# Attention in a four-layer kernel: the bonus turned from a contiguous tile, two value quarters and one copy moved in the order of the engines

## The chip, the cores and the metric

The kernel runs on one core of a Trainium2 chip (trn2). The metric is the device time of one execution in microseconds, the median of several runs. A profiled execution has a time of its own and a span (first to last instruction) inside it.

## The reference

Four layers, each with a layer norm ahead, a layer norm behind and a residual. Only the first one is touched by the change. It is an attention over B=32 sequences of T=256 positions, D=128, 16 heads with 4 numbers per key and 64 per value:

```
Q = normalize(x @ W_q.T); K = normalize(x @ W_k.T); V = x @ W_v.T      # per head
Qn = normalize(Q @ W_nudge); scores = Qn @ K.T * 0.5
s = sigmoid(3 * K @ simple_roots.T)                                   # 4 numbers a head and key
cw = products of s or 1-s for the 16 corners; k_bonus = cw . chamber_bonus[head]
scores += k_bonus[key]; causal mask; attn = softmax(scores); out = (attn @ V) @ W_out.T
x = x + layernorm(out)
```

The other layers are a gated feed-forward, a tanh recurrence and a mixture of 32 experts; they run after the attention in the same program and are the same in both kernels.

## The kernel before, in words

The attention works on one sequence (a block) at a time, and every engine runs the same software pipeline over blocks: step(b, f, n, m, z, y, par) does scores and weighted values for block b, the preparation of keys, queries and values for f = b+1, norm and the q/k projection for n = b+2, input statistics for m = b+3, the output projection for z = b-1 and the closing norm for y = b-2. The order on each engine is written out by hand, and the engines wait for each other by semaphores. The loop (Fori) holds two blocks in its body; six blocks at the start and five at the end are written out.

- TensorE (L568 to L645, in rounds' step): scores(b, p) for the head pairs p = 0 to 7 (L478), weighted(b, g) for the groups g = 0 to 3 (L500, with row sums L508), weighted(z, 3) between scores(b, 0) and scores(b, 1). Between them: the transposes of xn (L574), the q/k projection L586 from xnT, four quarters of the values, values(f, 0..3) (L551, three matmuls each, into the bank back), spread_out (L522), the turn of the bonus (L600, the matmul of k5_wide's fifth column with the identity), the turn of qkn (L613), the turn of the running maximum cmax (L620), the rotation L627, the turns of k_aug and q_aug (L560) and the output projection (L536).
- GpSimd: copy of the keys into k5 (L412), bonus() as a tree of eight, four, two and one products (L367 to L379), the last of which writes column 4 of k5_wide (a tile of 144 rows of 5 floats); the masks 0 to 7 (L323, an affine select over two heads pairs of probabilities), three of them between the steps of bonus(); split() of k5 and q5 into three bf16 parts (L332, L336), the rows of k_aug and q_aug (L423 to L451), and 1/sqrt of the variances (L350, L352).
- ScalarE: the exponentials, weights(b, h, h+1) (L655), copies of PSUM banks: copy_out (L665), copy_values (L673), xnT (L684), squares (L689), q_augT (L722), y_sb (L727).
- VectorE: reciprocal of the row sums of z and its bf16 parts (L788 to L797), sum of squares and three Newton steps (L828 to L760), normalise (L806), qkn (L840), bonT (L846: the turned bonus out of PSUM), the running maximum cmax over keys by a scan (L849), q5 (L855, L864) and the rest of the norms.

A score's key bonus and the query's running maximum are extra columns of k5 and q5. mask p waits for the exponentials of its two heads, weighted(b, g) waits for mask 2g+1, scores(b, p) waits for the exponentials of pair p-1, and reciprocal(z) waits for the sums of weighted(z, 3).

Of the kernel before, what the change touches and what calls it, by code (L numbers as in the profile page):

```python
# [14 lines left out]
P = 128  # L15
# [77 lines left out]
def attention_layer(nc, x, w_qk, w_v, w_rot, w_out, bonus0, bonus_step, x1_d, mix, mix_d, room, row_buf, sorted_d):  # L93

    with ExitStack() as ctx:
# [6 lines left out]
        def sem(name):  # L102
# [53 lines left out]
        q_augT = [sb(f"q_augT{i}", [P, GROUPS, T], BF16) for i in range(2)]  # L156
        k_augT = [sb(f"k_augT{i}", [P, GROUPS, T], BF16) for i in range(2)]
        bonT = sb("bonT", [HEADS, T])
        cmax = sb("cmax", [P, T])
        views = 10 * HID  # L160
        val = [room[:, views + i * SPAN:views + (i + 1) * SPAN].rearrange("p (i h v) -> p i h v", i=TT, h=HEADS)
               for i in range(2)]
# [31 lines left out]

        names = ("w", "const", "xa", "stat_a", "mv_a", "ve", "rstd", "xn", "p_xnT", "xnT", "p_qk", "sq1", "ss1",
                 "ssg1", "roots", "qkn", "p_qkT", "qkT", "p_rot", "sq2", "ek", "qraw", "ss2", "ssg2", "ek1",
                 "sg", "q4", "kcopy", "bon", "p_bonT", "bonT", "cmax", "p_cmax", "q5", "ksplit", "qsplit", "kaug",
                 "qaug", "p_kaT", "p_qaT", "kaT", "qaT", "p_v", "val", "p_score", "prob", "masked", "p_out", "raw",
                 "p_sum", "rec", "rec_high", "rec_rest", "rec_mid", "rec_parts", "rest_row", "wv_split", "low_sel", "back_row", "back_r", "xnT_high", "xnT_low", "p_bc", "onT", "p_y",
                 "y", "stat_y", "mv_y", "yn", "xr", "x1", "x1_out", "mix_w", "mix_split_v", "mix_split_g", "mix_const", "blank", "fill")  # L200
# [3 lines left out]
        BON = 11  # L204
        RSQ = 10
        N_IDENT = 4
        N_CONST = 22

        ctx.callback(clear, nc, list(s.values()))
        block = ctx.enter_context(nc.Block(no_gpsimd_drain=True))  # L210
# [68 lines left out]
        def _(pool):  # L279
# [11 lines left out]
            def late_constants():  # L291
                const(pool.memset(q_aug[:], 0.0))
                const(pool.memset(k5_wide[:], 0.0))
                const(pool.memset(cmax[:], 0.0))
                const(pool.memset(k_aug[:], 0.0))
                const(pool.memset(q_aug[:, :, 27:30], 1.0))
                const(pool.memset(k_aug[:, :, 24:27], 1.0))
                for row, fill, base in ((high_row, 1.0, 0), (mid_row, -1.0, -GROUPS), (low_row, -1.0, -2 * GROUPS)):

                    const(pool.memset(row[:], 0.0))  # L300
                    const(pool.affine_select(out=row[:].rearrange("p (g j) -> p g j", j=GH),
                                             in_=row[:].rearrange("p (g j) -> p g j", j=GH),
                                             compare_op=ALU.not_equal, fill=fill, base=base,
                                             pattern=[[-1, GROUPS], [-AUG, GH]], channel_multiplier=1))
                const(pool.memset(pick[:], 0.0))
                flat = pick[:].rearrange("p g c -> p (g c)")
                const(pool.memset(flat[:, 0:GROUPS * (AUG + 1) - AUG:AUG + 1], 1.0))
                for row in (GROUPS, 2 * GROUPS):
                    const(pool.memset(flat[:, row:row + GROUPS * (AUG + 1) - AUG:AUG + 1], 1.0))
                const(pool.memset(pick[:, :, 3 * GROUPS:], 1.0))  # L310
                pool.memset(row_buf[:], 0.0).then_inc(s["blank"], 1)
                pool.wait_ge(s["blank"], 1)
                pool.memset(row_buf[:, :, ROW_ID:ROW_ID + 1], 1.0).then_inc(s["blank"], 1)
                pool.wait_ge(s["w"], 96)
                const(pool.tensor_tensor(bond[:], bond[:], bon0[:], ALU.subtract))
# [38 lines left out]
            def bonus(n, between):  # L354

                wait_apart(pool, s["sg"], n + 1, s["const"])
                wait_apart(pool, s["p_bonT"], n, s["const"])
                def did(ins):
                    did.c += 1
                    ins.then_inc(s["bon"], 1)  # L360
                    wait_apart(pool, s["bon"], BON * n + did.c, s["const"])
                did.c = 0
                def sig(r, w):
                    return sg[:, :, :, r:r + 1].to_broadcast([P, TT, HEADS, w])
                step_b = bond[:].rearrange("p (o h) c -> p o h c", o=1).to_broadcast([P, TT, HEADS, 8])
                base_b = bon0[:].rearrange("p (o h) c -> p o h c", o=1).to_broadcast([P, TT, HEADS, 8])
                did(pool.tensor_tensor(bt[0][:], sig(0, 8), step_b, ALU.mult))  # L367
                did(pool.tensor_tensor(bv[0][:], bt[0][:], base_b, ALU.add))
                between(0)
                for r in range(1, 4):  # L370
                    pair = bv[r - 1][:].rearrange("p i h (c two) -> p (i h) c two", two=2)
                    w = 8 >> r
                    t = bt[r][:].rearrange("p i h c -> p (i h) c")
                    sr = sg[:].rearrange("p i h r -> p (i h) r")[:, :, r:r + 1].to_broadcast([P, TT * HEADS, w])
                    did(pool.tensor_tensor(t, pair[:, :, :, 1], pair[:, :, :, 0], ALU.subtract))
                    did(pool.tensor_tensor(t, t, sr, ALU.mult))
                    out = bv[r][:].rearrange("p i h c -> p (i h) c") if r < 3 \
                        else k5_wide[:, 0:TT * HEADS, DH:DH + 1]
                    did(pool.tensor_tensor(out, t, pair[:, :, :, 0], ALU.add))  # L379
                    if r != 2:  # L380
                        between(1 if r == 1 else 2)

# [24 lines left out]
            def step(b, f, n, m, z, y, par):  # L407
                if isinstance(m, int) and m == 1:
                    late_constants()
                if f is not None:  # L410
                    wait_apart(pool, s["qkn"], f + 1, s["const"])
                    pool.tensor_scalar(k5[:, :, :, 0:DH], qkn[:, :, HEADS:, :], 1.0, 0.0,  # L412
                                       ALU.mult, ALU.add).then_inc(s["kcopy"], 1)
                    bonus(f, lambda p: mask(b, p))
                    mask(b, 3)
                    wait_apart(pool, s["kcopy"], f + 1, s["const"])
                    wait_apart(pool, s["p_kaT"], f, s["const"])
                    split(k5, k_part, "ksplit", f)
                    wait_apart(pool, s["ksplit"], STEPS_K * (f + 1), s["const"])

                    kp = k_part[:].rearrange("p k r c -> p r k c")
                    rows = k_aug[:].rearrange("p r (m c) -> p r m c", c=DH)
                    pool.tensor_scalar(rows[:, :, 0:3, :], kp[:, :, :, 0:DH], 1.0, 0.0, ALU.mult, ALU.add)  # L423
                    pool.tensor_scalar(rows[:, :, 3:5, :], kp[:, :, 0:2, 0:DH], 1.0, 0.0, ALU.mult, ALU.add)
                    pool.tensor_scalar(rows[:, :, 5, :], kp[:, :, 0, 0:DH], 1.0, 0.0, ALU.mult, ALU.add)
                    pool.tensor_scalar(k_aug[:, :, 27:30], kp[:, :, :, DH], 1.0, 0.0,
                                       ALU.mult, ALU.add).then_inc(s["kaug"], 1)
                else:
                    for p in range(4):
                        mask(b, p)  # L430
                        if isinstance(b, int) and b == B - 1:
                            split_weight("h2", p)
# [27 lines left out]
        def _(pe):  # L460
# [104 lines left out]
            def step(b, f, n, m, z, y, par):  # L565
# [30 lines left out]
                if f is not None:  # L596
                    wait(pe, s["bon"], BON * (f + 1))
                    wait(pe, s["qaT"], f)
                    for i in range(TT):
                        mm = pe.matmul(turned[:, i * P:(i + 1) * P], k5_wide[:, i * HEADS:i * HEADS + P, DH], ident[:],  # L600
                                       start=True, stop=True)
                    mm.then_inc(s["p_bonT"], 1)
                values(f, par, 2)

                scores(b, par, 4)
                weighted(b, par, 1)
                scores(b, par, 5)

                spread_out(z, 1)
                if n is not None:  # L610
                    wait(pe, s["qkn"], n + 1)
# [1 line left out]
                        mm = pe.transpose(front[:, i * P:(i + 1) * P], qkn[:, i].rearrange("p h c -> p (h c)"),  # L613
                                          ident[:])
                    mm.then_inc(s["p_qkT"], 1)
                values(f, par, 3)
                if f is not None:
                    wait(pe, s["cmax"], f + 1)
                    for i in range(TT):
                        mm = pe.matmul(turned[:, T + i * HEADS:T + (i + 1) * HEADS], cmax[:, i * P:(i + 1) * P],  # L620
                                       ident[:, 0:HEADS], start=True, stop=True)
                    mm.then_inc(s["p_cmax"], 1)
                spread_out(z, 2)
                if n is not None:
                    wait(pe, s["qkT"], n + 1)
# [22 lines left out]
        def _(act):  # L648
# [27 lines left out]
            def step(b, f, n, m, z, y, par):  # L676
                weights(b, 0, 1)
                copy_out(z, 1 - par, 3)
                weights(b, 2, 3)

                if n is not None:
                    wait(act, s["p_xnT"], n + 1)
                    wait(act, s["p_v"], 4 * (n - 1))
                    act.activation(xnT[par][:], front[:, 0:T], ACT.Copy).then_inc(s["xnT"], 1)  # L684
                copy_values(f, par, 0)
                if n is not None:
                    wait(act, s["p_qk"], n + 1)
# [8 lines left out]
                copy_out(b, par, 0)  # L696
                weights(b, 6, 7)
                copy_values(f, par, 1)
                copy_values(f, par, 2)

                weights(b, 8, 9)
                copy_out(b, par, 1)
                weights(b, 10, 11)
                if n is not None:
                    wait(act, s["p_qkT"], n + 1)
                    act.activation(qkT[:], front[:, 0:T], ACT.Copy).then_inc(s["qkT"], 1)
# [1348 lines left out]
```

## Time and profile before

| | |
|---|---|
| median of 3 runs | 1771.08 us (1771.04 to 1773.08) |
| profiled execution | 1771.21 us |
| its span | 1769.4 us |
| busy share of the span: TensorE, its weight loads, VectorE, ScalarE, GpSimd | 93%, 70%, 75%, 50%, 57% |
| attention half | about the first 780 us |
| granted TensorE clock, mean | 0.973 |

How to read it: the share of an engine is an average over all layers. In a time line of one engine, each row is one instruction or a run of equal ones with its start and length; a note in brackets is the idle time ahead of it and what ended that. Starts of neighbouring matmuls overlap, so the time that a group holds TensorE is the distance from its start to the next group's start. Gaps below 0.15 us have no note.

### The profile page before, as it was taken

The page shows a single profiled execution, that of the slowest core. Times are in us where ns is not written, and L with a number is a line of the kernel's source. Part 1 is how long each engine was busy: PE and PEld are TensorE (multiplying, and loading weights), DVE is VectorE, ACT ScalarE, POOL GpSimd, SP SyncE. Part 2 cuts the span into 40 slices and gives each one's busy share as a digit, 9 for nine tenths or more (in the row PEclk, how much of TensorE's full clock was granted, in tenths as well). Part 3 has the DMA queues.
Part 4 walks back from the last instruction along what each step waited for, and adds up shares of the span by engine and source line. Part 5 has one row for each costly group of instructions (what it writes and reads, how often), then busy time and mean ns, then how long its engine had stood idle before and what let it go on. Part 6 is the DMA issues. An engine that isn't in the chain of part 4 may idle for free.

```text
span 1769.4 us, 47120 instructions
## 1 busy us (share of the span) xinstructions
PE 1639.8 (93%) x14871; PEld 1231.4 (70%) x14871; DVE 1318.6 (75%) x3869; ACT 889.9 (50%) x2003; POOL 1005.7 (57%) x1782
## 2 busy tenths in 40 slices
PE   3999999999999999859999999999999999689996
PEld 2677777777777777537778888878787886555553
DVE  5688888888888888645567777777777775758886
ACT  2666666666666666514444444444444443224443
POOL 5888888888888888722233333333333333327777
PEclk8999999999999999969999999999999999699998
DMA  1001111111111113010120000000000002534441
GB/s 42 11 29 55 54 54 54 54 54 54 54 54 54 54 54 104 14 36 13 50 81 22 31 28 29 27 30 29 26 30 28 26 25 75 178 123 133 133 132 41
DMA packets 78259, 95.96 MB, mean 54 GB/s; under 512 B 7046, under 2 KB 62995, under 8 KB 78160
## 3 DMA queue, kind: packets, MB, share of 16 engines
q1 hardware_dynamic: 70992, 77.91, 13.8%
q0 software_dynamic: 7168, 16.87, 2.7%
q8 instruction: 46, 0.75, 0.2%
q14 instruction: 53, 0.43, 0.1%
HBM read 53.14 MB, written 43.69 MB: 55 GB/s over the span
## 4 chain that ended last, share of the span: by engine, by line
PE 40%; DVE 7%; issue 4%; POOL 2%; DMA 1%; ACT 1%; DVEq 0%; POOLq 0%; SPq 0%; ACTq 0%
PE main L1329 6%; PE main L1331 5%; PE main L1338 5%; PE main L1487 4%; PE yp L1409 3%; PE xi L1244 2%; PE main L1269 2%; PE main L1282 2%; PE main L1393 2%; PE main L1396 1%; PE main L1394 1%; PE route L1501 1%; PE xi L1501 1%; PE turn L1237 1%; PE yp L1509 1%
## 5 line engine op out<-in xcount | busy, mean ns | idle before, releaser
L655 ACT ACTIVATE wgu<-score 128x384 f32<-128x384 f32 x512 | 223.2, 489 | 80.1 <-PE score L478 78.6
L1329 PE MATMUL main<-hT_high,h_high 128*128 128x512 f32 x512 | 221.2, 432 | 0.9 <-ACT hT_high L1586 0.9
L1331 PE MATMUL main<-hT_high,h_low 128*128 128x512 f32 x512 | 201.3, 393 | 0.0
L500 PE MATMUL outp<-wgu 128*32 128x256 f32 (+1 forms) x4096 | 194.5, 331 | 5.4 <-POOL wgu L323 4.3
L323 POOL TENSOR_SCALAR_AFFINE_SELECT wgu<-wgu 128x512 f32<-128x512 f32 x256 | 167.1, 658 | 46.1 <-ACT wgu L655 28.2
L500 PEld LDWEIGHTS outp<-wgu 128*32 128x32 f32 x4096 | 115.9, 110 | 70.6 <-issue 22.1
L1338 PE MATMUL main<-hT_low,h_high 128*128 128x512 f32 x512 | 138.3, 391 | 0.1
L1894 DVE SCALAR_TENSOR_TENSOR th<-th,main 128x512 f32<-128x512 f32 x64 | 43.9, 686 | 114.5 <-ACT th L1613 114.5
L536 PE MATMUL back<-wout,wgu 128*128 128x128 f32 x1024 | 128.6, 280 | 0.0
L536 PEld LDWEIGHTS back<-wout,wgu 128*128 128x128 f32 x1024 | 121.9, 195 | 0.4
L1227 POOL DMA_INDIRECT out<-res,idx x96 | 96.8, 1008 | 44.1 <-issue 40.5
L1244 PEld LDWEIGHTS xi<-state,wh_sb 128*128 128x128 f32 x512 | 93.1, 195 | 39.2 <-ACT state L1536 22.9
L1536 ACT ACTIVATE state<-xi,bias 128x32 f32<-128x32 f32 x256 | 73.2, 286 | 86.7 <-PE xi L1244 85.6
L1338 PEld LDWEIGHTS main<-hT_low,h_high 128*128 128x128 f32 x512 | 96.2, 188 | 21.8 <-DVE hT_low L1848 0.8
L508 PE MATMUL total<-wgu,pick 128*32 128x256 f32 (+1 forms) x2048 | 108.2, 329 | 0.0
L1170 POOL TENSOR_SCALAR bve_f<-bmv_f 128x4 f32<-128x4 f32 x16 | 7.7, 484 | 174.7 <-DVE bmv_f L1691 174.7
L1165 POOL TENSOR_TENSOR hT_low<-wgu,hT_high 128x512 fp32r<-128x512 f32 x64 | 83.0, 1297 | 42.0 <-ACT wgu L1578 41.4
L1329 PEld LDWEIGHTS main<-hT_high,h_high 128*128 128x128 f32 x512 | 97.0, 189 | 13.6 <-ACT hT_high L1586 1.4
L1577 ACT ACTIVATE hT_high<-main,sc 128x512 fp32r<-128x512 f32 x64 | 44.0, 688 | 124.0 <-PE main L1338 124.0
L1331 PEld LDWEIGHTS main<-hT_high,h_low 128*128 128x128 f32 x512 | 97.1, 190 | 11.7 <-issue 0.2
L1487 PE MATMUL main<-wgu,xgT 128*128 x192 | 100.2, 604 | 3.3 <-DVE hid_g L1947 2.4
L665 ACT ACTIVATE wgu<-outp 128x512 f32<-128x512 f32 x128 | 76.5, 598 | 48.1 <-PE outp L500 45.7
(295 smaller groups left out, 4353.9 us busy)
## 6 DMA issues: line engine op xcount, KB each, us to landing
sorted_d<-row_buf SPq DMA_DIRECT2D x26, 772.0 KB, 3.7
xg<-sorted_d SPq DMA_DIRECT2D x48, 386.0 KB
wgu<-in_gate_up SPq DMA_DIRECT2D x4, 2048.0 KB
xa<-in_x SPq DMA_DIRECT2D x32, 128.0 KB, 3.5
xr<-in_x SPq DMA_DIRECT2D x32, 128.0 KB, 3.3
x_d<-x SPq DMA_DIRECT2D x32, 128.0 KB, 1.8
x1c<-x_d SPq DMA_DIRECT2D x16, 256.0 KB, 2.7
x1v<-x_d SPq DMA_DIRECT2D x16, 256.0 KB, 2.7
```

What stands on the lines that cost most here:

```text
L323: pool.affine_select(out=blocks, in_=blocks, compare_op=ALU.is_ge, fill=0.0, base=0, pattern=[[0, 4], [1, P]], channel_multiplier=-1).then ...
L500: m = pe.matmul(outp[AUG * j:AUG * (j + 1), p % 2, k * P:T], val[par][:, k, h, v:v + AUG], weights(h, k), start=(k == 0), stop=(k == 1), t ...
L508: m = pe.matmul(total[AUG * j:AUG * (j + 1), k * P:T], pick[:, g, :], weights(GH * g + j, k), start=(g == 0 and k == 0), stop=(g == GROUPS ...
L536: m = pe.matmul(back[:, i * P:(i + 1) * P], onT[1 - par][:, c, i * P:(i + 1) * P], wout[:, c, :], start=(c == 0 and i == 0), stop=(c == PA ...
L655: act.activation(prob[:, h // 2 % (RING // 2), :, h % 2, :], score[h % BANKS][:, 0:SC].rearrange("p (c q) -> p c q", q=P), ACT.Exp).then_i ...
L1165: pool.tensor_tensor(hT_part[1][1][:, m, :], hT[1][:, m, :], hT_part[1][0][:, m, :].bitcast(F32), ALU.subtract).then_inc(s["h2_low"], 1)
L1227: pool.indirect_dma_start(out=out_rows[:, :], out_offset=bass.IndirectOffsetOnAxis(ap=idx[k][:, n:n + 1], axis=0), in_=res[k][:, n, :], in ...
L1244: pe.matmul(xi[:, o:o + B], wh_sb[:], state[:, prev:prev + B], start=False, stop=(t == STEPS - 1), skip_group_check=True).then_inc(s["p_st ...
L1329: pe.matmul(main[m % 2][:, :], w[0][:, k, m * P:(m + 1) * P], src[0][:, k, :], start=(k == 0), stop=False)
L1331: pe.matmul(main[m % 2][:, :], w[1][:, k, m * P:(m + 1) * P], src[0][:, k, :], start=False, stop=False)
L1338: mm = pe.matmul(main[m % 2][:, :], w[0][:, k, m * P:(m + 1) * P], src[1][:, k, :], start=False, stop=(k == HC - 1))
L1487: pe.matmul(main[2 * (r % 2) + i][:, :], xgT[r % 2][:, i * P:(i + 1) * P], wgu[:, bass.ds(e, 1), :].rearrange("p o i -> p (o i)"), start=T ...
```

## The change

On GpSimd, the last product of the bonus goes to a new tile bonus_row (144 contiguous floats a partition, zeroed at the start, so that there is one constant more), and a new tensor_scalar copies its 32 columns into column 4 of k5_wide, with a semaphore bon_k of its own that the k split waits for. On TensorE the turn of the bonus (L600) takes its weights from bonus_row; values(f, par, 2) moves from ahead of scores(b, par, 4) to behind scores(b, par, 5); values(f, par, 3) moves from ahead of the turn of cmax to behind it. On ScalarE the copy of xnT moves ahead of weights(b, 2, 3), and copy_values(f, par, 2) moves behind weights(b, 10, 11).

```diff
+        bonus_row = sb("bonus_row", [P, P + HEADS])
@@
-        N_CONST = 22
+        N_CONST = 23
@@ GpSimd
+                const(pool.memset(bonus_row[:], 0.0))
@@ GpSimd, bonus()
                     out = bv[r][:].rearrange("p i h c -> p (i h) c") if r < 3 \
-                        else k5_wide[:, 0:TT * HEADS, DH:DH + 1]
+                        else bonus_row[:, 0:TT * HEADS].rearrange("p (r o) -> p r o", o=1)
                     did(pool.tensor_tensor(out, t, pair[:, :, :, 0], ALU.add))
+                    if r == 3:
+                        pool.tensor_scalar(k5_wide[:, 0:TT * HEADS, DH], bonus_row[:, 0:TT * HEADS], 1.0, 0.0,
+                                           ALU.mult, ALU.add).then_inc(s["bon_k"], 1)
@@ GpSimd, step
                     wait_apart(pool, s["kcopy"], f + 1, s["const"])
+                    wait_apart(pool, s["bon_k"], f + 1, s["const"])
                     wait_apart(pool, s["p_kaT"], f, s["const"])
                     split(k5, k_part, "ksplit", f)
@@ TensorE, step
                     for i in range(TT):
-                        mm = pe.matmul(turned[:, i * P:(i + 1) * P], k5_wide[:, i * HEADS:i * HEADS + P, DH], ident[:],
+                        mm = pe.matmul(turned[:, i * P:(i + 1) * P], bonus_row[:, i * HEADS:i * HEADS + P], ident[:],
                                        start=True, stop=True)
                     mm.then_inc(s["p_bonT"], 1)
-                values(f, par, 2)
 
                 scores(b, par, 4)
                 weighted(b, par, 1)
                 scores(b, par, 5)
 
+                values(f, par, 2)
                 spread_out(z, 1)
@@ TensorE, behind the turn of qkn
-                values(f, par, 3)
                 if f is not None:
                     wait(pe, s["cmax"], f + 1)
@@
                     mm.then_inc(s["p_cmax"], 1)
+                values(f, par, 3)
                 spread_out(z, 2)
@@ ScalarE, step
                 copy_out(z, 1 - par, 3)
-                weights(b, 2, 3)
-
                 if n is not None:
                     wait(act, s["p_xnT"], n + 1)
                     wait(act, s["p_v"], 4 * (n - 1))
                     act.activation(xnT[par][:], front[:, 0:T], ACT.Copy).then_inc(s["xnT"], 1)
+                weights(b, 2, 3)
+
                 copy_values(f, par, 0)
@@
                 copy_values(f, par, 1)
-                copy_values(f, par, 2)
 
                 weights(b, 8, 9)
                 copy_out(b, par, 1)
                 weights(b, 10, 11)
+                copy_values(f, par, 2)
```

## Rows read from the trace of the kernel before

**Rows 1.** Busy time (instructions) by engine, TensorE clock and DMA, block A's window
```profile
core 0: us, PE busy (x) PEld busy (x) DVE busy (x) ACT busy (x) POOL busy (x), PEclk, DMA share, GB/s
379.87:402.42 22.55, 22.18 (x318) 16.29 (x314) 19.01 (x45) 14.52 (x34) 18.75 (x42) 1.00 0.17 57
```
**Rows 2.** Time line of TensorE in block A: start us, length us, engine, line, operation
```profile
379.87 0.34 PE L478 MATMUL score<-q_augT,k_augT 32*128 32x256 bf16 x4
380.14 0.44 PE L574 MATMUL front<-ident,xn 128*128 128x128 f32 x2
...
381.44 0.71 PE L586 MATMUL front<-wqk,xnT 128*128 128x128 f32 x4 [0.17 <-ACT xnT L684]
...
382.62 1.51 PE L500 MATMUL outp<-wgu 128*32 128x256 f32 x32 [0.20 <-POOL wgu L323]
...
386.01 1.05 PE L600 MATMUL turned<-ident,k 128*128 128x128 f32 x4
386.82 0.48 PE L551 MATMUL back<-wv_high,xnT_high 128*128 128x512 f32 x1
...
387.96 1.51 PE L500 MATMUL outp<-wgu 128*32 128x256 f32 x32
...
390.06 0.34 PE L478 MATMUL score<-q_augT,k_augT 32*128 32x256 bf16 x4
...
390.69 0.48 PE L551 MATMUL back<-wv_high,xnT_high 128*128 128x512 f32 x1
...
391.47 0.51 PE L620 MATMUL turned<-ident,cmax 128*128 128x16 f32 x4
```
**Rows 3.** Time line of VectorE in blocks A and B
```profile
380.10 1.76 DVE L788 RECIPROCAL rec<-total 128x256 f32<-128x256 f32 x1 [0.78 <-PE total L508]
...
386.13 0.70 DVE L758 TENSOR_TENSOR root_t<-sums,root 128x96 f32<-128x96 f32 x1
...
390.12 0.95 DVE L849 TENSOR_TENSOR_SCAN cmax<-bonT 16x256 f32<-16x256 f32 x1
...
402.60 1.76 DVE L788 RECIPROCAL rec<-total 128x256 f32<-128x256 f32 x1 [1.07 <-issue]
...
408.31 0.26 DVE L758 TENSOR_TENSOR root_t<-sums,root 128x96 f32<-128x96 f32 x1
...
412.08 0.96 DVE L849 TENSOR_TENSOR_SCAN cmax<-bonT 16x256 f32<-16x256 f32 x1
```
**Rows 4.** Time line of TensorE in block B and at its end
```profile
413.75 0.51 PE L620 MATMUL turned<-ident,cmax 128*128 128x16 f32 x4
...
424.69 0.34 PE L478 MATMUL score<-q_augT,k_augT 32*128 32x256 bf16 x4
```
**Rows 5.** Time line of GpSimd in blocks A and B
```profile
381.85 0.64 POOL L323 TENSOR_SCALAR_AFFINE_SELECT wgu<-wgu 128x512 f32<-128x512 f32 x1 [0.31 <-POOL bv L379]
...
385.33 1.39 POOL L323 TENSOR_SCALAR_AFFINE_SELECT wgu<-wgu 128x512 f32<-128x512 f32 x2 [0.31 <-POOL k L379]
...
404.04 0.64 POOL L323 TENSOR_SCALAR_AFFINE_SELECT wgu<-wgu 128x512 f32<-128x512 f32 x1 [0.31 <-POOL bv L379]
...
408.36 0.70 POOL L323 TENSOR_SCALAR_AFFINE_SELECT wgu<-wgu 128x512 f32<-128x512 f32 x1 [0.20 <-ACT wgu L655]
```
**Rows 6.** All instructions of L600, L620, L788: duration ns min/median/max, first and last start
```profile
L600 PEld LDWEIGHTS turned<-ident,k x128: 295/316/321, 28.6 to 722.1; 128*128 128x128 f32 x128
L620 PEld LDWEIGHTS turned<-ident,cmax x128: 187/192/333, 34.2 to 727.0; 128*128 128x128 f32 x128
L788 DVE RECIPROCAL rec<-total x32: 1757/1758/1758, 66.7 to 760.1; 128x256 f32<-128x256 f32 x32
```
**Rows 7.** Groups of GpSimd instructions, 200 to 700 us: busy us, mean ns, idle
```profile
L412 POOL TENSOR_SCALAR k<-qkn 128x128 f32<-128x128 f32 x22 | 6.6, 301 | 0.0
```
**Rows 8.** Time line of ScalarE in block A
```profile
380.24 0.87 ACT L655 ACTIVATE wgu<-score 128x384 f32<-128x384 f32 x2 [0.29 <-PE score L478]
381.00 0.39 ACT L684 ACTIVATE xnT<-front 128x256 f32<-128x256 f32 x1
381.31 0.60 ACT L673 ACTIVATE wgu<-back 128x512 f32<-128x512 f32 x1
```

More of the change, by code:

```diff
@@ L196, in attention_layer @@
                  "ssg1", "roots", "qkn", "p_qkT", "qkT", "p_rot", "sq2", "ek", "qraw", "ss2", "ssg2", "ek1",
-                 "sg", "q4", "kcopy", "bon", "p_bonT", "bonT", "cmax", "p_cmax", "q5", "ksplit", "qsplit", "kaug",
+                 "sg", "q4", "kcopy", "bon", "bon_k", "p_bonT", "bonT", "cmax", "p_cmax", "q5", "ksplit", "qsplit", "kaug",
                  "qaug", "p_kaT", "p_qaT", "kaT", "qaT", "p_v", "val", "p_score", "prob", "masked", "p_out", "raw",
```

## Prediction

> **What bounds the kernel now.** The change touches only the attention half, the first 780 us of the profiled execution. I read first the busy time of one stretch of the attention loop, then the time lines of TensorE, VectorE, GpSimd and ScalarE in two neighbouring blocks. The loop body holds two blocks, and they differ a little: block A runs from 379.87 to 402.42 us (22.55 us), block B from 402.42 to 424.69 us (22.27 us), both counted from the matmuls of scores(b, 1), a point that I call S1. Their mean is 22.41 us; the ends of the window in [rows 1] are two neighbouring S1. TensorE is busy for 22.18 of the 22.55 us of block A. What the reader is to see in its time line [rows 2] is how small its named waits are: 0.17 us for xnT ahead of L586 and 0.20 us for mask 1 ahead of weighted(0). In a loop this tight the question is which ring of waits has the least slack. There are three.
>
> TensorE alone: 22.27 us in block B, with the xnT wait in it.
>
> VectorE and TensorE: the reciprocal L788 waits for the sums that end just ahead of S1. It starts 0.23 us behind S1 in A and 0.18 us in B, and VectorE then works almost without a gap to the end of the running maximum L849, which is at 390.12+0.95 = 391.07 us in A and 412.08+0.96 = 413.04 us in B [rows 3]. That is S1+11.20 and S1+10.62. TensorE takes that maximum at L620, at 391.47 and 413.75 us, S1+11.60 and S1+11.33 [rows 2, 4]. From there to the next S1 TensorE needs 402.42-391.47 = 10.95 us in A and 424.69-413.75 = 10.94 us in B. So this ring has a slack of a few tenths only: 0.4 us in A and 0.7 us in B, less what it takes from the maximum to the first matmul.
>
> GpSimd: in its time line nearly every gap is a wait for its own last result, as the 0.31 us ahead of mask 2 in A. The one clear wait for another engine is 0.20 us ahead of mask 3 in B [rows 5]. Two blocks take 44.82 us, so its own work fills (44.82-0.20)/2 = 22.31 us a block. GpSimd is nearly as tight as TensorE.
>
> **The turn of the bonus from a contiguous tile.** The weight loads of L600, which step over five floats, take 316 ns; those of L620, contiguous and of the same size, take 192 ns [rows 6]. L600's four instructions now hold TensorE for 386.82-386.01 = 0.81 us [rows 2]. With loads of 192 ns I scale that by 192/316 and get 0.49, a saving of 0.32 us a block; the bounds are 0 and 4*(316-192) ns = 0.50 us. On TensorE's own path that would be 32*0.32 = 10.2 us. But it lies between S1 and L620, the stretch that the VectorE chain covers, so it only makes TensorE arrive earlier at a wait.
>
> **The copy back into k5 on GpSimd.** One tensor_scalar of 128x32. L412, the same operation on 128x128, has a mean of 301 ns [rows 7]; L379 to mask 2 has a gap of 0.31 us [rows 5] that comes from two waits in a row, and the copy sits between these two. Its cost is between 0 (hidden by the second wait) and 0.30 us; I take 0.05 us, since the copy is a quarter of L412's size and the second wait is worked off while it runs. Its wait bon_k ahead of the split has behind it the k split, k_aug and with it the turn of k_aug on TensorE, but it is passed during mask 3 (about 0.65 us of work), so it costs 0. By the forecast below GpSimd gets 0.5 us of slack a block, so even 0.30 us would not reach the end. The extra memset (128x144) runs once at the start, 0 to 0.3 us; I take 0.
>
> **The turned input ahead of exponentials 2 and 3.** The exponentials now start at 380.24 us, S1+0.37 [rows 8]. The transposes of xn end at 380.14+0.44 = 380.58 us [rows 2], so xnT can start at about S1+0.78 and takes 0.31 us of ScalarE's time (from 381.00 to the next start at 381.31; its record says 0.39). The two exponentials then run from S1+1.09 to S1+1.96. Mask 1, which needs them, can start at S1+2.09 (0.13 us for the semaphore, as from the end of mask 1 at 382.49 to weighted(0) at 382.62) and ends at S1+2.73. Now it ends at S1+2.62 in A and S1+2.26 in B [rows 5]. So this move takes away the 0.17 us wait at L586 and puts weighted(0) at S1+2.86, 0.1 to 0.4 us later than now. Both lie under the VectorE chain as well.
>
> **Quarter 2 of the values one block of scores later, quarter 3 behind the maximum.** The first swaps places only: one quarter goes from ahead of weighted(1) to behind scores(5). The second, which the short name of the change doesn't mention, is the one that counts: values(f, 3) goes from ahead of L620 to behind it. A quarter takes 391.47-390.69 = 0.78 us [rows 2]. TensorE reaches L620 earlier by that, where the maximum isn't ready, and has 0.78 us more to do behind it.
>
> **The sum.** A new block is: S1 to the end of the maximum, then to the first matmul of L620, then the rest. From the end of the maximum to L620 I take 0.26 us (0.13 us for the semaphore and 0.13 us of the first weight load of 0.19 us, which nothing hides now; bounds 0.1 and 0.4 us). The rest is the present one plus 0.78 us. Block A: 11.20+0.26+10.95+0.78 = 23.19 us, 0.64 us more than now. Block B: 10.62+0.26+10.94+0.78 = 22.60 us, 0.33 us more. The mean is +0.485 us. The reciprocals are 32 [rows 6]; the last three belong to blocks in which the next-but-one input is missing and VectorE's chain is short, so 29 blocks count: 29*0.485 = +14.1 us. The profiled execution took 1771.2 us (its span 1769.4 us and 1.8 us around it), the median of the runs is 1771.1 us, so the two bases are the same within 0.1 us. 1771.2+14.1 = **1785.3 us**.
>
> **What may make the VectorE chain longer or shorter.** It is the same list of instructions in A and B and yet takes 10.97 us in one and 10.44 us in the other. The same L758 takes 0.70 us where it starts beside a GpSimd mask and 0.26 us elsewhere [rows 3]. I see about 1.3 us of such lengthening in A and 0.8 us in B, so the chain lies between 9.65 and some 11.3 us, by how it falls against GpSimd's masks and splits. The Trainium skill ("SBUF — State Buffer", SBUF: two separate sides) calls the port pair that the two engines share an exclusive lock, given to whichever instruction starts first, the other fully blocked; the trace agrees with its 0.70 against 0.26 us.
>
> **The rivals.** (1) The collisions get worse. With mask 1 from S1+2.09 on, masks 2 and 3 begin near S1+5.6 and S1+6.35, and the root steps, which run from S1+5 to S1+8, meet both masks and the first subtraction of the split. Each meeting costs 0.2 to 0.5 us, which gives every block at least A's chain: 23.0 to 23.2 us, +0.6 to +0.8 us, 1788.6 to 1794.4 us. The page's lock is the rule by which this goes, and by it both blocks would get the longer chain.
> (2) No change. If the chain loses nearly all of its collisions (9.65 us), its ring falls to 0.23+9.65+0.26+11.73 = 21.87 us and others bind. TensorE by way of exponentials 2 and 3: weighted(0) at S1+2.86; weighted(1) 4.24 us later by TensorE's work (387.96-382.62 = 5.34, less 0.78, less 0.32) and, by mask 3, 4.36 us behind the end of mask 1, so S1+7.1; scores(5) 2.10 us later and L620 another 1.41 us later [rows 2], S1+10.6; with 11.73 us that is 22.35 us. GpSimd's own 22.31+0.05 = 22.36 us agrees. So 22.35 us, -0.06*29 = -2 us, 1769.5 us.
> (3) Faster. If besides that GpSimd's lengthened steps shrink by 0.2 us and the exponentials come 0.15 us earlier than I reckon, the block is 22.2 us: -0.2*29 = -6 us, 1765 us. A full gain of TensorE's 0.32+0.17 us a block (14 us, 1757 us) would need all rings to give way. Against both stands GpSimd's work of 22.31 us.
> (4) The turn isn't faster from a contiguous tile. Then TensorE reaches L620 at S1+10.9 instead of S1+10.6, still at the maximum or 0.1 us behind it in B: 1785 to 1788 us. The 192 ns of L620's loads speak against it.
>
> **How the numbers follow.** A measurement of this kernel can tell about 0.2% (3.5 us) from no change. Forecast, 1779 to 1789 us: 0.50. Rival 1: 0.17. Rival 4: 0.05. Rival 2: 0.17. Rival 3: 0.11. The faster side is rival 3 (0.11), no change is rival 2 without a tail and the low edge of the forecast (0.15), the rest is slower (0.74). The range must reach over rival 2 and most of rival 1: 1768 to 1795 us.
>
> **What would show it.** In the trace after, TensorE should have an idle time ahead of L620 that ends with VectorE's running maximum, 0.3 to 0.8 us in every block; the distance from that matmul to the next S1 should be 11.7 us; mask 1 should wait for the exponentials; GpSimd should show waits for ScalarE ahead of mask 0; weight loads of the bonus turn should be near 192 ns. The forecast is wrong if the maximum ends before S1+10.4 us, so if the chain sheds its collisions, or if the stretch behind L620 grows by less than 0.78 us because something in it was waiting unseen.

## The result and the profile after

The changed kernel takes 1787.65 us (median of 4 runs, 1782.7 to 1789.6), the kernel before 1771.06 us beside it; the ratio is 1.0091, with a 95% interval of 1.0075 to 1.0106. It is slower, by 16.6 us. Its profiled execution took 1782.7 us with a span of 1780.6 us.

The change touches the attention half only, so the cleanest measure is the time from the first to the last y_sb copy, one per block. Its row for the kernel before and for the changed one (minimum, median and maximum length in ns, then first and last start in us):

```profile
L727 ACT ACTIVATE y_sb<-back x32: 384/384/385, 86.8 to 774.5; 128x256 f32<-128x256 f32 x32
```
```profile
L733 ACT ACTIVATE y_sb<-back x32: 384/384/386, 86.1 to 788.0; 128x256 f32<-128x256 f32 x32
```

That is 687.7 us before and 701.9 us after, +14.2 us; the forecast was +14.1 us. The other 2.4 us of the 16.6 us can't be placed: they are less than what the time outside these copies scatters by. The same changed kernel, profiled again, had 702.1 us between the copies and 1787.7 us in all, against 701.9 and 1782.7 us. The two traced runs, before and changed, differ by 1782.7-1771.2 = 11.5 us only.

In the changed kernel a block takes 22.91 to 22.96 us from one S1 (the matmuls of scores(b, 1)) to the next, 22.93 us on the mean of six, against 22.41 us. TensorE's time line after, the block that starts at 386.52 us, answers to [rows 2]:

```profile
386.52 0.34 PE L484 MATMUL score<-q_augT,k_augT 32*128 32x256 bf16 x4
...
387.78 0.71 PE L592 MATMUL front<-wqk,xnT 128*128 128x128 f32 x4
388.55 0.34 PE L484 MATMUL score<-q_augT,k_augT 32*128 32x256 bf16 x4
389.46 1.51 PE L506 MATMUL outp<-wgu 128*32 128x256 f32 x32 [0.58 <-POOL wgu L325]
...
392.86 0.61 PE L606 MATMUL turned<-ident,bonus_row 128*128 128x128 f32 x4
393.40 0.34 PE L484 MATMUL score<-q_augT,k_augT 32*128 32x256 bf16 x4
393.71 1.51 PE L506 MATMUL outp<-wgu 128*32 128x256 f32 x32
...
397.11 0.38 PE L619 MATMUL front<-ident,qkn 128*128 128x128 f32 x2
397.63 0.62 PE L625 MATMUL turned<-ident,cmax 128*128 128x16 f32 x4
398.10 0.48 PE L557 MATMUL back<-wv_high,xnT_high 128*128 128x512 f32 x1
...
409.48 0.34 PE L484 MATMUL score<-q_augT,k_augT 32*128 32x256 bf16 x4
```

The reader is to see three things. The wait for xnT ahead of the projection (now L592) is gone, and a wait of 0.58 us for mask 1 ahead of weighted(0) stands in its place. The turn of the bonus holds TensorE for 393.40-392.86 = 0.54 us instead of 0.81 us. And between the turn of qkn and the turn of the maximum there is a hole: 397.11 to 397.63 us, where the two transposes of qkn hold TensorE for 0.14 us. VectorE's time line, which answers to [rows 3], shows what ends it:

```profile
386.75 1.76 DVE L794 RECIPROCAL rec<-total 128x256 f32<-128x256 f32 x1 [1.21 <-PE total L514]
...
392.35 0.74 DVE L764 TENSOR_TENSOR root_t<-sums,root 128x96 f32<-128x96 f32 x1
393.12 0.57 DVE L765 SCALAR_TENSOR_TENSOR root_u<-root_t,root 128x96 f32<-128x96 f32 x1
...
396.69 0.88 DVE L855 TENSOR_TENSOR_SCAN cmax<-bonT 16x256 f32<-16x256 f32 x1
```

The maximum ends at 396.69+0.88 = 397.57 us, S1+11.05, and TensorE's turn of it starts 0.06 us later. From there to the next S1 are 409.48-397.63 = 11.85 us, against 10.95 us in [rows 2, 4]. The waits of the weight loads from 200 to 700 us say the same for all 22 blocks (columns: waiting line, what it waited for, us in total, times, longest):

```profile
PEld outp L506 <- POOL wgu L325: 9.8, 22, 0.7
PEld turned L625 <- DVE cmax L855: 9.1, 22, 0.5
```

GpSimd, which answers to [rows 5], now waits for the exponentials ahead of mask 1, and its new copy L383 stands ahead of masks 2 and 3:

```profile
388.63 0.71 POOL L325 TENSOR_SCALAR_AFFINE_SELECT wgu<-wgu 128x512 f32<-128x512 f32 x1 [0.64 <-ACT wgu L661]
...
391.65 0.25 POOL L381 TENSOR_TENSOR bonus_row<-bt,bv 128x32 f32<-128x32 f32 x1
392.07 0.35 POOL L383 TENSOR_SCALAR k<-bonus_row 128x32 f32<-128x32 f32 x1 [0.16 <-POOL bonus_row L381]
392.35 1.24 POOL L325 TENSOR_SCALAR_AFFINE_SELECT wgu<-wgu 128x512 f32<-128x512 f32 x2
```

### The profile page after: what moved, and what is told of

It reads as the page before. It is cut to its first block, busy times and chain, and to the rows that moved or that the text cites. A ratio compares the mean times of both kernels' runs of the same rounds, so it can differ in the third digit from the quotient of the medians.

```text
span 1780.6 us, 47200 instructions
## 1 busy us (share of the span) xinstructions
PE 1638.3 (92%) x14871; PEld 1216.1 (68%) x14871; DVE 1317.0 (74%) x3869; ACT 888.9 (50%) x2003; POOL 1013.5 (57%) x1815
## 4 chain that ended last, share of the span: by engine, by line
PE 40%; DVE 7%; issue 4%; POOL 2%; DMA 1%; ACT 1%; DVEq 0%; POOLq 0%; SPq 0%; ACTq 0%
PE main L1335 6%; PE main L1337 5%; PE main L1344 5%; PE main L1493 4%; PE yp L1415 3%; PE xi L1250 2%; PE main L1275 2%; PE main L1399 2%; PE main L1288 2%; PE main L1402 1%; PE main L1400 1%; PE route L1507 1%; PE xi L1507 1%; PE yp L1515 1%; PE turn L1243 1%
## 5 line engine op out<-in xcount | busy, mean ns | idle before, releaser
L506 PE MATMUL outp<-wgu 128*32 128x256 f32 (+1 forms) x4096 | 196.1, 333 | 17.0 <-POOL wgu L325 14.1
L325 POOL TENSOR_SCALAR_AFFINE_SELECT wgu<-wgu 128x512 f32<-128x512 f32 x256 | 163.5, 648 | 49.8 <-ACT wgu L661 49.6
L812 DVE TENSOR_TENSOR wgu<-spread,wgu 128x512 f32<-128x512 f32 x128 | 86.8, 678 | 34.4 <-PE spread L528 29.2
```

Of the source, the lines that this page charges most:

```text
L325: pool.affine_select(out=blocks, in_=blocks, compare_op=ALU.is_ge, fill=0.0, base=0, pattern=[[0, 4], [1, P]], channel_multiplier=-1).then ...
L506: m = pe.matmul(outp[AUG * j:AUG * (j + 1), p % 2, k * P:T], val[par][:, k, h, v:v + AUG], weights(h, k), start=(k == 0), stop=(k == 1), t ...
L812: dve.tensor_tensor(o, spread[:], o, ALU.mult).then_inc(s["onT"], 1)
```

## The experiments

A ring is here a chain of waits that comes back to its own start one block later, so the block can't be shorter than it; the longest ring sets the block. Two reasons could explain the loss, and the profile after shows a wait for each: theory 1, the ring of VectorE's running maximum, which got the 0.78 us of quarter 3 behind it; theory 2, the copy of xnT ahead of exponentials 2 and 3, which delays mask 1. The first four runs take each alone and each away. "Block" is the mean of six or more S1 distances near 300 to 460 us, and "first to last copy" is that of y_sb; both are of the one traced run of each kernel. The ratio is to the kernel before as run beside each; its median was between 1769.8 and 1771.1 us, and medians of different rows compare only as closely as that.

| kernel | median us | ratio to before (95%) | block us | first to last copy us |
|---|---|---|---|---|
| before | 1771.06 | | 22.41 | 687.7 |
| changed | 1787.65 | 1.0091 (1.0075 to 1.0106) | 22.93 | 701.9 |
| quarter 3 behind the maximum, alone | 1778.92 | 1.0055 (1.0039 to 1.0072) | 22.67 | 694.9 |
| changed, quarter 3 put back | 1786.84 | 1.0093 (1.0076 to 1.0110) | 22.89 | 704.0 |
| copy of xnT moved, alone | 1780.01 | 1.0049 (1.0032 to 1.0066) | 22.68 | 697.8 |
| changed, copy of xnT put back | 1781.19 | 1.0052 (1.0032 to 1.0072) | 22.68 | 695.3 |
| quarter 2 moved, alone | 1786.65 | 1.0090 (1.0073 to 1.0107) | 22.91 | 703.8 |
| turn from the contiguous tile, alone | 1766.91 | 0.9981 (0.9972 to 0.9991) | 22.39 | 685.5 |
| changed, one Newton step less | 1776.44 | 1.0035 (1.0020 to 1.0049) | 22.55 | 691.0 |
| the same, copy of xnT put back | 1764.28 | 0.9957 (0.9942 to 0.9973) | 22.14 | 680.3 |
| turn alone, copies into k5 on ScalarE | 1780.10 | 1.0055 (1.0037 to 1.0073) | 22.68 | 694.3 |
| the same, projection later | 1779.36 | 1.0049 (1.0030 to 1.0068) | 22.75 | 697.4 |
| changed, maximum ahead of normalise | 1784.92 | 1.0089 (1.0068 to 1.0111) | 22.65 | 695.7 |
| changed, again | 1787.07 | 1.0093 (1.0074 to 1.0112) | 22.92 | 702.1 |

**Quarter 3 of the values alone.**

```diff
-                values(f, par, 3)
                 if f is not None:
                     wait(pe, s["cmax"], f + 1)
@@
                     mm.then_inc(s["p_cmax"], 1)
+                values(f, par, 3)
                 spread_out(z, 2)
```

> The kernel before with one edit: values(f, 3) behind the turn of the maximum. Theory 1 (the VectorE ring: TensorE waits for the running maximum and has 0.78 us more to do behind it): block A 11.20+0.06+10.95+0.78+0.11 = 23.1 us, block B 22.5 us, mean +0.4 us a block, 29 blocks, so 1779 to 1786 us, with TensorE idle ahead of the maximum's turn. Theory 2 (the loss comes from the copy of xnT ahead of exponentials 2 and 3, which delays mask 1): nothing changes here, 1770 to 1773 us.

Measured: 1778.92 us, +8.9 us, just below theory 1's range and well above theory 2's. The blocks alternate between 22.46 and 22.87 us, for which theory 1 had said 22.5 and 23.1. The turn of the maximum starts 0.05 to 0.08 us behind the end of the scan in all of them, as here at 393.42+0.94 = 394.36 us:

```profile
393.42 0.94 DVE L849 TENSOR_TENSOR_SCAN cmax<-bonT 16x256 f32<-16x256 f32 x1
394.41 0.62 PE L619 MATMUL turned<-ident,cmax 128*128 128x16 f32 x4 [0.18 <-DVE cmax L849]
```

So the move has a price of its own, and it is that ring's.

**Quarter 3 put back in the changed kernel** (the same edit reversed).

> The changed kernel with values(f, 3) put back ahead of the turn of the maximum, all else changed. Theory 1: the VectorE ring falls to about 22.1 us and no longer binds; what is left is weighted(0) at S1+2.92 and 19.5 us of TensorE's work from there to the next S1, 22.4 us a block, so 1770 to 1774 us. Theory 2: mask 1 is as late as in the changed kernel and the loss stays, 1783 to 1789 us.

Measured: no gain at all, 22.89 us a block. By its number theory 2 had this right, but its reason is only a part of it. The maximum ends at S1+11.04 and TensorE turns it only at S1+12.0, so the ring of theory 1 is loose here; mask 1 and weighted(0) are where they were. In between stands a wait that neither theory had. TensorE's time line:

```profile
395.82 0.50 PE L557 MATMUL back<-wv_high,xnT_high 128*128 128x512 f32 x1
...
396.87 0.38 PE L619 MATMUL front<-ident,qkn 128*128 128x128 f32 x2
397.49 0.50 PE L557 MATMUL back<-wv_high,xnT_high 128*128 128x512 f32 x1 [0.23 <-ACT wgu L679]
```

and ScalarE's:

```profile
395.93 0.87 ACT L661 ACTIVATE wgu<-score 128x384 f32<-128x384 f32 x2 [0.29 <-PE score L484]
396.83 0.60 ACT L679 ACTIVATE wgu<-back 128x512 f32<-128x512 f32 x1
```

Quarters 2 and 3 go into the one bank back. With quarter 2 behind scores(5), quarter 3 follows it on TensorE after 1.2 us, but ScalarE copies quarter 2 out only behind exponentials 10 and 11, at 396.83+0.60 = 397.43 us. Quarter 3 starts 0.06 us after that, and 0.48 us after TensorE could (0.14 us behind the turn of qkn at 396.87). This is theory 3, the bank. The ring through it begins with mask 1, so the late copy of xnT is in it too: weighted(0) starts 0.27 us later than in the kernel before on the mean, the bank adds 0.48 us behind it, and the faster turn takes 0.27 us away. That makes the 0.48 us by which this block is longer than 22.41 us.

**The copy of xnT alone.**

```diff
                 copy_out(z, 1 - par, 3)
-                weights(b, 2, 3)
-
                 if n is not None:
...
                     act.activation(xnT[par][:], front[:, 0:T], ACT.Copy).then_inc(s["xnT"], 1)
+                weights(b, 2, 3)
```

> The kernel before with one edit: the copy of xnT ahead of exponentials 2 and 3. Theory 2: weighted(0) starts at S1+2.9 instead of S1+2.75 and S1+2.48, and from there TensorE needs 19.80 us to the next S1 as before, 22.7 us a block, +0.3 us, so 1777 to 1782 us. Theory 1 alone: the copy lies under the VectorE chain and costs nothing, 1770 to 1773 us.

Measured: as theory 2 said, 22.62 and 22.74 us, with weighted(0) at S1+2.82 and S1+2.94. In the kernel as it was, this copy is worth 0.27 us a block.

**The copy of xnT put back in the changed kernel** (the same edit reversed).

> The changed kernel with the copy of xnT back behind exponentials 2 and 3. Theory 1: the maximum still ends near S1+11.05 and sets the block, 22.8 to 23.1 us, so 1783 to 1790 us, as the changed kernel; only the wait ahead of weighted(0) shrinks and the one ahead of the maximum's turn grows by as much. Theory 2: weighted(0) comes 0.3 us earlier and so does all behind it, 1776 to 1780 us.

Measured: 22.47 and 22.89 us, a gain of 0.25 us a block. The median of 1781.19 us lies in neither range, above theory 2's 1776 to 1780 us and below theory 1's 1783 to 1790 us. Theory 2's number is the nearer one, but VectorE's ring sets both kernels: here, too, the turn of the maximum follows the scan at once, after a wait that has grown to 0.51 us. What differs is the end of the scan: S1+10.57 and S1+10.99 in turn, instead of S1+11.00 and S1+11.05. So nearly all of the gain is in the short blocks. This is VectorE's chain in one of them (S1 at 361.86 us), and below it GpSimd's masks 1, 2 and 3:

```profile
364.23 0.48 DVE L798 SCALAR_TENSOR_TENSOR rec_rest<-rec_high,rest_sel,rec 128x256 f32<-128x256 bf16 x1
...
367.08 0.57 DVE L766 SCALAR_TENSOR_TENSOR root<-root_u,root 128x96 f32<-128x96 f32 x1
367.68 0.26 DVE L764 TENSOR_TENSOR root_t<-sums,root 128x96 f32<-128x96 f32 x1
367.98 0.57 DVE L765 SCALAR_TENSOR_TENSOR root_u<-root_t,root 128x96 f32<-128x96 f32 x1
```

```profile
363.41 0.64 POOL L325 TENSOR_SCALAR_AFFINE_SELECT wgu<-wgu 128x512 f32<-128x512 f32 x1 [0.31 <-ACT wgu L661]
...
366.90 0.64 POOL L325 TENSOR_SCALAR_AFFINE_SELECT wgu<-wgu 128x512 f32<-128x512 f32 x1
367.80 0.64 POOL L325 TENSOR_SCALAR_AFFINE_SELECT wgu<-wgu 128x512 f32<-128x512 f32 x1 [0.26 <-ACT wgu L661]
```

In the changed kernel L798 takes 0.73 us, beside mask 1, and the second L764 takes 0.74 us, beside mask 2 (392.35+0.74 = 393.09 us in the fence above). Here they take 0.48 and 0.26 us, and L766 is long instead with 0.57 us. In the trace of the changed kernel from 200 to 700 us, 44 of 198 root steps (L764 to L766) take 0.57 to 0.74 us, and every one of them ends 0.11 us behind the end of a mask; 44 take 0.31 to 0.43 us and end 0.11 to 0.12 us behind a GpSimd step of the bonus or the split; the other 110 take 0.26 us. So the traces show that GpSimd's instructions hold these steps up, the masks most of all, and the move of mask 1 changes which of them meet.

**Quarter 2 of the values alone.**

```diff
-                values(f, par, 2)
 
                 scores(b, par, 4)
                 weighted(b, par, 1)
                 scores(b, par, 5)
 
+                values(f, par, 2)
                 spread_out(z, 1)
@@
-                copy_values(f, par, 2)
                 weights(b, 8, 9)
                 copy_out(b, par, 1)
                 weights(b, 10, 11)
+                copy_values(f, par, 2)
```

> The kernel before with one edit: values(f, 2) behind scores(b, 5) and its copy behind exponentials 10 and 11. Theory 3 (the bank: quarters 2 and 3 now follow each other on TensorE, and the one bank between them must be copied out by ScalarE first, behind the exponentials): from weighted(1) to the turn of the maximum 4.8 us as in the run with quarter 3 undone, instead of 3.5 us and the 0.9 us of the quarter, so +0.4 us a block, 1780 to 1785 us. Rival (the order is only swapped): 1770 to 1773 us.

Measured: +16 us, as much as the whole change loses, from one swap, at 22.89 and 22.93 us a block, a little above theory 3's 1780 to 1785 us. From weighted(1) to the turn of the maximum are 11.94-7.13 = 4.81 us. Its waits of TensorE from 200 to 700 us:

```profile
PE back L551 <- ACT wgu L673: 5.1, 22, 0.2
```

So this edit, done alone, costs 0.50 us a block by the bank. In the changed kernel quarter 3 stands behind the maximum and the bank is free in time; there it is the maximum that binds, and at nearly the same length. Putting quarter 3 back exchanges this wait for the bank's. The changed kernel with quarter 2 put back was not run.

**The turn from the contiguous tile alone** (bonus_row, the copy L383 and the semaphore bon_k of the change; no move).

> The kernel before with one edit: the bonus turned from bonus_row, with the copy back on GpSimd. If TensorE's own work set the block, the 0.27 us saved at the turn would show, 29 times: 1763 us. If GpSimd's ring binds, as the masks in its time line say, its 22.31 us get 0.14 us for the copy, and the block stays at 22.4 to 22.45 us: 1770 to 1773 us.

Measured: between the two forecasts. It is faster than before by 0.19%, and the whole interval lies below 1; the traces have 2.2 us of it between the first and last y_sb copy. The blocks wander between 22.12 and 22.58 us. Weighted(0) waits for mask 1 in 11 of 22 blocks, as in the kernel before, but for 3.5 us in total instead of 2.1 us; that fits a load by GpSimd's copy, though it wasn't tried alone. Of the kernels that leave nothing out, only this one beats the kernel before.

**VectorE's chain made shorter in the changed kernel** by one Newton step. The kernel leaves that step out, so its norms are less exact; it is a means to measure and no improvement. What reads the third step's result reads the second's here (not shown).

```diff
-        RSQ = 10
+        RSQ = 7
@@
-                for i in range(3):
+                for i in range(2):
```

> The changed kernel with two Newton steps instead of three in the inverse roots (the third step is left out, so the norms are less exact); VectorE's chain is shorter by three instructions, 0.9 to 1.3 us. Theory 1 (VectorE's chain sets the changed kernel's block): the block falls from 22.94 us to the next ring, weighted(1) at S1+7.2 plus 3.5 us plus 11.73 us = 22.45 us, at most 22.6 us: 1772 to 1778 us. Theory 2 alone (mask 1 sets it): no change, 1783 to 1789 us.

Measured: 10.6 us less than the changed kernel as run on another chip, 22.49 and 22.61 us. The maximum now ends at S1+9.72 to S1+9.86, 0.95 us before TensorE takes it, and what is left is the wait for mask 1:

```profile
PE outp L506 <- POOL wgu L325: 11.5, 22, 0.6
```

So VectorE's chain does set the changed kernel's block, and behind it by 0.4 us stands the next ring.

**The same with the copy of xnT put back.**

> The run before with the copy of xnT back behind exponentials 2 and 3 as well (again without the third Newton step). Both waits are gone then: TensorE could do 21.9 us a block, and GpSimd's own work of 22.31+0.14 us is what is left: 22.4 to 22.5 us, 1769 to 1774 us. If GpSimd is not a bound, 21.9 to 22.1 us and 1756 to 1762 us.

Measured: 1764.28 us, between the two ranges, with 22.10 and 22.19 us a block. With both waits gone the only named wait ahead of TensorE's matmuls is the 0.17 us for xnT. The floor of 22.31 to 22.5 us that I had given GpSimd doesn't exist: I had added up its steps at the lengths that they had in the kernel before, and they aren't fixed (there, the last L336 of a block took 0.77 us in one block and 0.49 us in another).

**Both copies into k5 on ScalarE**, from the kernel with the turn alone.

```diff
@@ both copies leave GpSimd's program (not shown); ScalarE, step
                 weights(b, 0, 1)
+                if f is not None:
...
+                    act.activation(k5[:, :, :, 0:DH], qkn[:, :, HEADS:, :], ACT.Copy).then_inc(s["kcopy"], 1)
                 copy_out(z, 1 - par, 3)
@@
                 copy_values(f, par, 1)
+                if f is not None:
+                    wait(act, s["bon"], BON * (f + 1))
+                    act.activation(k5_wide[:, 0:TT * HEADS, DH], bonus_row[:, 0:TT * HEADS],
+                                   ACT.Copy).then_inc(s["bon_k"], 1)
                 copy_values(f, par, 2)
```

> The kernel before with the bonus turned from bonus_row, and both copies into k5 (keys and bonus column) moved from GpSimd to ScalarE: keys behind exponentials 0 and 1, the column behind copy_values(f, 1). If GpSimd's ring bound the run with the turn alone (block 22.41 us), it is now 0.27+0.14 us shorter than there and TensorE's own 22.1 us is what is left: -0.3 us a block against the kernel before, 1760 to 1765 us. If it was something else, 1766 to 1768 us as that run.

Measured: a miss, 13 us more than the kernel it starts from. GpSimd has two instructions less, but its k split now waits 0.30 us a block for the column from ScalarE, and everything behind it is later:

```profile
411.64 0.32 POOL L334 TENSOR_SCALAR k_part<-k 128x160 bf16<-128x160 f32 x1 [0.30 <-ACT k L707]
```

That delay comes round by a fourth ring, which the traces show but no run took apart: GpSimd's square root of the variances, VectorE's yn, ScalarE's y_sb copy, the exponentials 0 and 1 behind it, mask 0. The y_sb copy waits for yn in all 22 blocks, 19.8 us in total. ScalarE's time line:

```profile
402.65 0.38 ACT L737 ACTIVATE y_sb<-back 128x256 f32<-128x256 f32 x1 [0.86 <-DVE yn L910]
402.93 0.87 ACT L655 ACTIVATE wgu<-score 128x384 f32<-128x384 f32 x2
```

**The projection behind scores(b, 2) as well**, with its squares behind exponentials 4 and 5 (ScalarE's part not shown).

```diff
+                scores(b, par, 2)
                 if n is not None:
...
                     mm.then_inc(s["p_qk"], 1)
-                scores(b, par, 2)
                 weighted(b, par, 0)
```

> The run before, and L586 (q/k projection) behind scores(b, 2) on TensorE, its squares on ScalarE behind exponentials 4 and 5, so that nothing waits for xnT. TensorE saves the 0.2 to 0.3 us of that wait if mask 1 is in time (it ends near S1+2.2 to 2.4, weighted(0) could start at S1+2.2): block 21.9 to 22.1 us, 1754 to 1763 us. If mask 1 binds, no gain over the run before.

Measured: no gain, 22.75 us a block. The wait for xnT is gone and the one for mask 1 has grown to 16.8 us in 22 blocks, as its second forecast said.

**The changed kernel with the maximum ahead of VectorE's first normalise**, nothing left out, beside **the changed kernel again**.

```diff
                 roots(n, f)
-                normalise(z, par, 0)
@@ behind the scan
+                normalise(z, par, 0)
                 normalise(z, par, 1)
@@ TensorE, behind values(f, par, 2)
-                spread_out(z, 1)
@@ TensorE, behind the turn of cmax
+                spread_out(z, 1)
                 values(f, par, 3)
```

> The changed kernel with nothing left out, but VectorE's running maximum ahead of its first normalise, and spread_out(z, 1) behind the turn of the maximum. VectorE's chain to the maximum is 0.69+0.19 us shorter. Theory 1: as with one Newton step less, the block falls from 22.94 to 22.5 to 22.6 us, 1773 to 1779 us. If the maximum did not set the block, 1784 to 1790 us.

> The changed kernel as it is, beside the others on this chip: a block of 22.94 us, 1783 to 1790 us. It gives the base for the run with the maximum first.

Measured: in the trace the block falls from 22.92 to 22.65 us and the time between the copies by 6.4 us, as it should if the maximum set it. But the median is a miss: it falls by only 2.2 us, to 1784.92 us, which lies in the range given for a maximum that did not set the block and not in the 1773 to 1779 us of theory 1. The traced run was the fastest of four, from 1780.5 to 1788.6 us, and why the others gained less is open. That the maximum set the block rests on the run with one Newton step less, where all five runs gain; the changed kernel again behaved as expected. The scan now ends 0.4 us before TensorE takes it, and weighted(0) waits for mask 1 as with the shorter chain, with the moved spread_out(z, 1) as 0.3 us more work behind the turn.

## Why the prediction was right

The size and the main mechanism were right: 1785.3 us forecast, 1787.65 us measured, 14.1 against 14.2 us in the half that changes. That the two agree so closely is luck. The steps:

- **The sum.** End of the maximum at S1+11.20 and S1+10.62, taken over from before: measured 11.05 and 11.00, 0.12 us more on the mean. From there to the first matmul 0.26 us: measured 0.06 us. Behind it 10.95+0.78 = 11.73 us: measured 11.85 us, because the four matmuls after the wait hold TensorE for 398.10-397.63 = 0.47 us instead of 0.36 us. The errors of +0.12, -0.20 and +0.12 us nearly cancel, and leave a block that is 0.52 us longer where 0.485 us was forecast.
- **The 29 blocks.** At 0.52 us they would give 15.1 us, and the 29 distances from the first S1 to the last grew by 15.5 us in all. Between the y_sb copies it is 14.2 us because the first copy comes two blocks behind the first S1 (0.9 us of the growth) and the stretch behind the last S1 is 0.4 us shorter.
- **The turn**, 0.32 us: measured 0.27 us, with loads of 192 ns. It was said to be covered; in the changed kernel it is, and alone it brings 0.2%.
- **The copy on GpSimd**, 0.05 us: from L381's end to mask 2 it was 0.31 us and is 392.35-391.90 = 0.45 us, so 0.14 us. The second wait hides less of it.
- **The copy of xnT**, "both lie under the VectorE chain as well": this step failed. Its own numbers were good (xnT at S1+0.78, measured 0.82; mask 1's end at S1+2.73, measured 2.77 and 2.81), but the cover wasn't one. The chain that was to cover the later masks got longer by them, by 0.43 us in every second block and 0.06 us in the others. That is rival 1's mechanism, in one block of two, and 0.25 us a block on the mean; the forecast for those blocks had kept the short chain.
- **Quarter 2**, "swaps places only": this step failed too. It counted the instructions and not the bank that quarter 3 needs next. The loss stayed out of the forecast because quarter 3 moved as well and the two rings have the same length within 0.04 us.
- **Rival 2's floors.** GpSimd's 22.36 us fell with the run at 22.14 us. TensorE's ring by way of exponentials 2 and 3 is real: with the Newton step left out it sets the block, at 22.55 us where 22.35 us was reckoned.

So the total came out closer than its parts: 0.2 us too much ahead of the maximum's turn made up for the longer chain, and the ring that I had missed, the bank, runs beside the one that I had, where the longest counts and not the sum.

## What to carry to other kernels

Where every engine is nearly full, find the rings of waits and write the slack of each; moving work behind a wait lengthens that ring by all of the work, and the block by what exceeds the ring's slack (0.78 us moved, 0.26 us a block here). A matmul group that moves next to another one on the same bank needs the copy between them as near as the matmuls are. And undo one edit at a time before blaming one: here three edits cost 0.25 to 0.5 us a block each alone and 0.52 us together, and the only one that helps was hidden by them.

## What the runs showed of the hardware

VectorE's root steps of 128x96 took 0.26 us or up to 0.74 us, by what GpSimd did beside them. In the changed kernel's trace all 44 that took 0.57 us or more ended 0.11 us behind the end of a 128x512 mask. VectorE's chain of 21 instructions up to the maximum ended at S1+10.6 or S1+11.0 in the blocks of one kernel. GpSimd's 128x32 copy took 0.35 us in the changed kernel's blocks shown above and 0.25 us with the copy of xnT put back. Two runs of the changed kernel with 702 us between the copies took 1782.7 us at a mean granted clock of 0.976 and 1787.7 us at 0.972. That is 5 us, more than the turn alone gains; the clock goes with it, but that it is the cause was not tried.
